# A transformer block on one core: the context as a tile of 128 and a doubled 64, queries and keys rounded ahead of the sums' inverse, both ends reordered

## The chip, the cores and the metric

The kernel runs on one core of one Trainium2 chip. The metric is the device time in microseconds (us) of one execution; a lower time is better. TensorE (PE) has a separate unit for its weight loads (PEld); VectorE is DVE, ScalarE is ACT, GpSimd is POOL, SyncE is SP.

## The reference

For 4 batch rows with 512 tokens of width 256, and a context of 512 tokens of width 192:

```python
attn_in = _adaln(x, cond, ln1_w, ln1_b, ...)
x = _attn(attn_in, attn_in, sa_wq, sa_wkv, sa_wo, sa_bo) + x      # self
cross_in = _adaln(x, cond, ln1_w, ln1_b, ...)
ctx_n = _ln(context, ca_lnc_w, ca_lnc_b)
x = _attn(cross_in, ctx_n, ca_wq, ca_wkv, ca_wo, ca_bo) + x       # cross
ffn_in = _adaln(x, cond, ln2_w, ln2_b, ...)
x = gelu(ffn_in @ ff_w1 + ff_b1) @ ff_w2 + ff_b2 + x
```

`_attn` has 16 heads of 64, rotates queries and keys by position, and takes a softmax over all 512 keys. All of it is float32.

## The kernel before, in words

Most products are made of float32r halves: an operand is written as a rounded high half and a low half (the difference), and a product is three matmuls, high by high, high by low and low by high (`parts`). Queries, keys, the normed activations, the context, the weights and the attention's output are split so. ACT writes the high halves (`high_qk`, `high_o`), DVE or POOL the low ones (`low_qk`, `low_o`, `norm_split`, `low_weights`).

The attention runs in 64 periods, one for each pair of heads of a batch row: two pairs of one batch row make a quad u, and 4 quads (one for each batch row) share one set of weights w. Quads 0 to 15 are self-attention (periods 0 to 31), quads 16 to 31 cross-attention. Each engine has its own hand-written order (`period(p)`), and semaphores tie them. In period p:

- PE scores pair p, four blocks of keys (`score`, L813 to L819: two row halves of the array, one for each head), and between the blocks multiplies queries and keys of pair p+1 for their row maxima (`peak`, L848); then the column sums of the exponentials of pair p-1 (`total`, L860), the average of the values for pair p (`average`, L872), and the projections for later pairs: one job of queries or keys (`project`, job p+4; even jobs are keys and fall in even periods), in odd periods the values of the next quad (`project_v`), in even periods the output projection of the quad that ended (`project_out`, which waits for `low_o(p-1)` of the same period).
- ACT takes the exponentials (L548), the inverse of the sums of pair p-1 by a logarithm and an exponential (`guess_inverse`, L554 and L556), the high half of queries and keys of pair p+2 (`high_qk`, L562), and the high half of the output of pair p-1 (`high_o`, L574).
- DVE takes the row maxima (L1065), corrects the inverse and multiplies (`normalise`, L1070 to L1075, which start once ACT has the inverse), writes the low half of that output (`low_o`, L1079), then the low half of queries and keys of pair p+2 (`low_qk`, L1083: both inputs in SBUF), the products with the rotation table (`rotate`, L1092) and the residual additions (L1109).
- POOL adds the exponentials of pair p (`add_probs`, L415 and twice L420: all in SBUF), does halves of weights and norms, additions of bias rows (`add_bias`, L437) and the rotation's sums (L429, L430). SP lands the rotated queries and keys by DMA (`land`) and the row maxima (`land_max`).

In cross-attention the 192 context channels are two tiles of 96 rows (CK = 96), so that a key job has 2 halves x 2 tiles x 3 = 12 matmuls of 512 columns, and a quad's values 4 x 2 x 3 = 24 matmuls of 256 columns. 16 layer norms (4 of the context) are strewn over the periods: statistics in one (L1050), rows in the next, transposes on PE in the one of `turned_in`. Ahead of the periods stand the first norms and projections, behind them the two-layer network (`mlp`) for the four batch rows.

## Time and profile before

| | |
|---|---|
| median of 3 runs | 1116.58 us (1114.38 to 1116.66) |
| profiled execution, its own time | 1118.88 us |
| its span | 1117.1 us |
| PE busy | 1097.2 us, 98% |
| DVE / POOL / ACT busy | 858.1 / 775.7 / 636.9 us |
| mean granted PE clock | 0.994 |

The span goes from the first to the last instruction of the profiled execution; its own time has 1.8 us more, for what lies around. A timeline gives each instruction, or a run of like ones, with its start and its length in us; in brackets stands how long the engine sat idle before it and what ended that. Lines of the kernel are written L813.

### The profile page before, as it was taken

How to read it: one execution, taken by the hardware profiler on the slowest of the kernel's cores; microseconds unless marked ns; L12 is line 12 of the kernel's file. 1: busy time of each engine (PE TensorE's matmuls, PEld its weight loads, DVE VectorE, ACT ScalarE, POOL GpSimd, SP SyncE). 2: the span in 40 equal slices, each digit the busy share in tenths (PEclk: the TensorE clock that was granted, in tenths of full speed). 3: DMA queues.
4: the chain of work that ended last, by engine and by line, in shares of the span. 5: the costliest groups of instructions: out<-in, count | busy, mean ns of one | idle time of the engine just before them, and what ended most of it. 6: DMA issues, size and time to landing. Idle time of an engine off the chain costs nothing.

```text
span 1117.1 us, 18312 instructions
## 1 busy us (share of the span) xinstructions
PE 1097.2 (98%) x6904; PEld 785.1 (70%) x6904; DVE 858.1 (77%) x1023; ACT 636.9 (57%) x895; POOL 775.7 (69%) x503
## 2 busy tenths in 40 slices
PE   8989999999999999999999999999999999989998
PEld 7657666776666776666766667766666776756997
DVE  5878887878787777878888777777877777788554
ACT  6465565665666555577665555555555545775521
POOL 2687887787788767789799766777777667755210
PEclk9899999999999999999999999999999999999999
DMA  6312121311231111211121112211121111300001
GB/s 175 86 46 57 32 53 39 89 30 30 53 77 38 39 36 23 72 39 39 29 63 38 39 39 59 51 23 36 38 72 39 37 31 30 114 1 1 20 19 38
DMA packets 59606, 52.31 MB, mean 47 GB/s; under 512 B 23040, under 2 KB 42496, under 8 KB 59264
## 3 DMA queue, kind: packets, MB, share of 16 engines
q1 hardware_dynamic: 57632, 49.57, 18.5%
q10 hardware_dynamic: 1888, 1.59, 0.5%
q8 instruction: 55, 0.90, 0.3%
q14 instruction: 31, 0.25, 0.1%
HBM read 15.22 MB, written 2.10 MB: 16 GB/s over the span
## 4 chain that ended last, share of the span: by engine, by line
PE 90%; DVE 5%; ACT 2%; issue 1%; DMA 1%; SPq 0%; POOL 0%; ACTq 0%; POOLq 0%; DVEq 0%
PE ps L872 18%; PE ps L713 12%; PE ps L715 11%; PE ps L714 11%; PE ps L813 6%; PE ps L860 6%; PE ps L848 5%; PE ps L819 5%; PE ps L815 5%; PE ps L817 5%; PE ps L963 4%; DVE lo L1083 1%; PE ps L729 1%; DMA x<-x_dram 1%; DVE w_lo L1117 1%
## 5 line engine op out<-in xcount | busy, mean ns | idle before, releaser
L548 ACT ACTIVATE probs<-ps 128x1024 f32<-128x1024 f32 x256 | 262.5, 1027 | 208.0 <-PE ps L819 183.6
L1065 DVE TENSOR_REDUCE neg_max<-ps 128x2 f32<-128x1024 f32 x256 | 301.6, 1226 | 76.7 <-PE ps L848 76.7
L420 POOL TENSOR_TENSOR acc<-acc,probs 128x1024 f32<-128x1024 f32 x128 | 306.2, 2392 | 18.6 <-POOL acc L415 0.4
L872 PE MATMUL ps<-probs,v 128*64 128x512 f32 x1024 | 230.7, 592 | 0.0
L415 POOL TENSOR_TENSOR acc<-probs 128x1024 f32<-128x1024 f32 x64 | 153.2, 2394 | 72.1 <-ACT probs L548 72.1
L872 PEld LDWEIGHTS ps<-probs,v 128*64 128x64 f32 x1024 | 73.9, 137 | 146.1 <-issue 146.1
L429 POOL TENSOR_TENSOR eo<-tmp 128x512 f32<-128x512 f32 x63 | 89.7, 1424 | 120.2 <-DVE tmp L1092 120.1
L1092 DVE TENSOR_TENSOR tmp<-ps,rope 128x1024 f32<-128x1024 f32 x126 | 148.2, 1211 | 4.5 <-PE ps L715 4.3
L813 PE MATMUL ps<-max_rows,pick 64*128 64x512 f32 x512 | 109.3, 419 | 2.6 <-DVE o_lo L1079 1.6
L713 PE MATMUL ps<-xn_hi,w_hi 128*128 128x512 f32 x256 | 107.8, 421 | 2.5 <-DVE o_lo L1079 1.3
L848 PE MATMUL ps<-hi 64*128 64x512 f32 x512 | 104.8, 400 | 5.4 <-DVE neg_max L1065 2.6
L819 PE MATMUL ps<-hi,lo 64*128 64x512 f32 x512 | 104.0, 396 | 0.0
L715 PE MATMUL ps<-xn_hi,w_lo 128*128 128x512 f32 x256 | 102.8, 402 | 0.0
L815 PE MATMUL ps<-hi 64*128 64x512 f32 x512 | 102.7, 392 | 0.0
L817 PE MATMUL ps<-lo,hi 64*128 64x512 f32 x512 | 102.4, 390 | 0.0
L714 PE MATMUL ps<-xn_lo,w_hi 128*128 128x512 f32 x256 | 102.0, 398 | 0.0
L1083 DVE TENSOR_TENSOR lo<-lo,hi 128x1024 fp32r<-128x1024 f32 x64 | 98.3, 1535 | 0.0
L1070 DVE SCALAR_TENSOR_TENSOR ps<-ps,inv 128x512 f32<-128x512 f32 x64 | 44.8, 700 | 68.6 <-ACT inv L556 68.6
L580 ACT COPY v<-ps 128x512 f32<-128x512 f32 x64 | 37.4, 589 | 100.5 <-PE ps L715 100.5
L848 PEld LDWEIGHTS ps<-hi 64*128 64x128 f32 x512 | 81.0, 306 | 17.8 <-issue 5.2
L430 POOL TENSOR_TENSOR eo<-tmp 128x512 f32<-128x512 f32 x63 | 81.3, 1291 | 0.0
L713 PEld LDWEIGHTS ps<-xn_hi,w_hi 128*128 128x128 f32 x256 | 49.0, 192 | 45.4 <-issue 33.9
(116 smaller groups left out, 2250.0 us busy)
## 6 DMA issues: line engine op xcount, KB each, us to landing
lo<-eo SPq DMA_DIRECT2D x126, 256.0 KB, 3.2
w_raw<-pack_dram SPq DMA_DIRECT2D x16, 192.0 KB, 3.9
x<-x_dram SPq DMA_DIRECT2D x4, 512.0 KB, 7.5
w_raw<-pack_dram SPq DMA_DIRECT2D x8, 256.0 KB, 4.3
max_rows<-neg_max SPq DMA_DIRECT2D x128, 2.0 KB, 2.0
w_raw<-w_dram SPq DMA_DIRECT2D x2, 1024.0 KB, 5.8
out<-x SPq DMA_DIRECT2D x8, 256.0 KB, 2.2
ctx_in<-ctx_dram SPq DMA_DIRECT2D x4, 384.0 KB, 4.2
```

Source lines behind the costliest of these rows:

```text
L420: pool.tensor_tensor(acc[:, g % 2, :, :], acc[:, g % 2, :, :], probs[:, i, :, :], ALU.add).then_inc(added, 1)
L548: act.activation(probs[:, i, :, :], score_ps(i), ACT.Exp, scale=SCALE).then_inc(exped, 1)
L713: pe.matmul(out, a_hi, b_hi, start=first, stop=False)
L714: pe.matmul(out, a_hi, b_lo, start=False, stop=False)
L715: return pe.matmul(out, a_lo, b_hi, start=False, stop=last)
L813: pe.matmul(out[:, h, :], pick[half[h], :], max_rows[half[h], :], start=True, stop=False)
L815: pe.matmul(out[:, h, :], k_hi[half[h], cut], q_hi[half[h], :], start=False, stop=False)
L817: pe.matmul(out[:, h, :], k_hi[half[h], cut], q_lo[half[h], :], start=False, stop=False)
L819: mm = pe.matmul(out[:, h, :], k_lo[half[h], cut], q_hi[half[h], :], start=False, stop=True)
L848: mm = pe.matmul(out[:, h, :], hi[half, g % 2, 0, cut], hi[half, g % 2, 1, :], start=True, stop=True)
L872: mm = pe.matmul(av_ps[DH * h:DH * h + DH, :], v[:, u % 2, kt, c:c + DH], probs[:, kt, h, :], start=(kt == 0), stop=(kt == TT - 1))
L1065: dve.tensor_reduce(neg_max[:, g % 2, :, i], peak_ps(i), AX.X, ALU.max, negate=True).then_inc(maxed, 1)
```

## The change

It does these things. (1) The context's 192 channels become one tile of 128 rows and one of 64; the 64 are laid down twice, at rows 0 to 63 and 64 to 127, so that two products with the 64 can stand in the two row halves of the array (`project_rest` for keys, ahead of `total`; `project_v_rest` for values, behind the other projections). Context norms have four more ACT instructions each, weights of cross-attention 11 loads in place of 7, and several PSUM banks are dealt out anew. (2) In every period ACT does `high_qk(p + 2)` ahead of `guess_inverse(p - 1)`, and DVE does `low_qk(p + 2)` ahead of `normalise(p - 1)`. (3) At the start job 3 is cut in four pieces between the maxima of pair 0 (`project_3`), `land_max(0)` goes ahead of `land(2)`, the low half of pair 1 moves to POOL, and the first four bias additions move to periods 13 to 21. (4) At the end the scores of pair 62 no longer wait for the output before them, the split of the network's weights is one DVE instruction for each matrix instead of four, and DVE takes one of the last additions of exponentials from POOL.

```diff
-LOADS = (5, 7)
+LOADS = (5, 11)
...
+        def is_wide(u):
+            return QUADS // 2 <= u < QUADS - 1
+
+        def v_ps(u, tt):
+            if is_wide(u):
+                return ps[:, ((6, 7), (2, 3))[tt % 2][tt // 2], 0:D]
+            return ps[:, (3 if u == QUADS - 1 else 5) + tt // 2, tt % 2 * D:(tt % 2 + 1) * D]
...
+        def av_ps(g):
+            return ps[:, 5 if g == PAIRS - 3 else 1, :]
...
+        def is_rest(j):
+            return j % 2 == 0 and j >= JOBS // 2
+
+        def out_ps(u, r):
+            if u == QUADS - 1:
+                return last_ps[r]
+            return ps[:, (3 if is_job(2 * u + 6) and is_rest(2 * u + 6) else 5, 6)[r], :]
...
-        bias_in.update({0: 0, 1: 1, 5: 2, 7: 3})
+        bias_in.update({13: 0, 15: 1, 18: 2, 21: 3})
...
+                        first, second = KT * 128, KT * 128 + 256
+                        for rows, kt, src, at in ((slice(0, CK), 0, slice(0, CK), first),
+                                                  (slice(CK, 128), 0, slice(0, 128 - CK), second),
+                                                  (slice(0, 64), 1, slice(128 - CK, CK), second),
+                                                  (slice(64, 128), 1, slice(128 - CK, CK), second)):
+                            sp.dma_start(raw[rows, 1:3, kt, a, :],
+                                         pack[src, at:at + 256].rearrange("p (m c) -> p m c", m=2))\
...
             land(1)
+            land_max(0)
             land(2)
-            land_max(0)
             load_x(3)
...
+            pool.wait_ge(qk_high, 2)
+            pool.tensor_tensor(lo[:, 1, :, :], raw_qk[:, 1, :, :], hi[:, 1, :, :], ALU.subtract).then_inc(qk_low_1, 1)
...
+                    if order[n][0] == C:
+                        act.activation(z[:, tt, DC:D], src[:, tt, 128:DC], ACT.Identity, bias=centre[:, tt:tt + 1],
+                                       scale=rstd[:, tt:tt + 1])
+                    act.activation(z[:, tt, 0:src.shape[-1]], src[:, tt, :], ACT.Identity, bias=centre[:, tt:tt + 1],
...
                         exp(p, i)
+                if is_pair(p + 2):
+                    high_qk(p + 2)
                 if is_pair(p - 1):
                     guess_inverse(p - 1)
                 if p in rows_in_period:
                     norm_rows(rows_in_period[p])
...
+            def project_rest(j):
+                w, b, _ = quad(j // 2)
+                pe.wait_ge(maxed, 4 * (j - 3) + 3)
+                pe.wait_ge(w_split, 4 * w + 1)
+                pe.wait_ge(ln_split, 2 * norm_of(C, 1, b) + 2)
+                for n, (w_, a_) in enumerate(((w_hi, ctx_hi), (w_hi, ctx_lo), (w_lo, ctx_hi))):
+                    for e, half in enumerate(halves):
+                        c = slice(256 + e * 128, 256 + (e + 1) * 128)
+                        pe.matmul(job_ps(j, e), w_[half, 1, c], a_[half, b, 1, :], start=(n == 0), stop=False)
...
+            def project_v(u):
...
+                    for kt in range(1 if phase == 1 else KT):
+                        c = slice(kt * 256, (kt + 1) * 256)
+                        for n, (a_, w_) in enumerate(((a_hi, w_hi), (a_hi, w_lo), (a_lo, w_hi))):
+                            mm = pe.matmul(v_ps(u, tt), a_[:, b, kt, cut], w_[:, 2, c],
+                                           start=first and kt == 0 and n == 0, stop=(phase == 0 and kt == KT - 1 and n == 2),
+                                           skip_group_check=True)
...
+            def project_v_rest(u):
+                b = quad(u)[1]
                 for t in range(2):
-                    cut = slice((2 * r + t) * 128, (2 * r + t + 1) * 128)
-                    for kt in range(KT):
-                        c = slice(kt * 256, (kt + 1) * 256)
-                        mm = parts(v_ps(u, r)[:, t * D:(t + 1) * D], a_hi[0:rows, b, kt, cut], a_lo[0:rows, b, kt, cut],
-                                   w_hi[0:rows, 2, c], w_lo[0:rows, 2, c], kt == 0, kt == KT - 1)
-                mm.then_inc(v_projected, 1)
+                    for n, (a_, w_) in enumerate(((ctx_hi, w_hi), (ctx_hi, w_lo), (ctx_lo, w_hi))):
+                        for r, half in enumerate(halves):
+                            cut = slice((2 * r + t) * 128, (2 * r + t + 1) * 128)
+                            mm = pe.matmul(v_ps(u, 2 * r + t), a_[half, b, 1, cut], w_[half, 2, 256:512],
+                                           start=False, stop=(n == 2), skip_group_check=True)
+                            if n == 2 and (t == 1 if not is_wide(u) else r == 1):
+                                mm.then_inc(v_projected, 1)
...
-                    if g > 0:
+                    if g > 0 and g != PAIRS - 2:
                         pe.wait_ge(av_kept, g)
-                    if g > 1:
+                    if g > 1 and g != PAIRS - 2:
                         pe.wait_ge(o_low, g - 1)
...
+                if is_job(p + 4) and is_rest(p + 4):
+                    project_rest(p + 4)
...
+                if p in v_in and quad(v_in[p])[2] == 1:
+                    project_v_rest(v_in[p])
...
+            project_v(0)
             project(2)
             modulate(2)
             peak(0, 0)
             peak(0, 1)
             modulate(3)
+            project_3(0, 0)
             peak(0, 2)
+            project_3(0, 1)
             peak(0, 3)
+            project_3(1, 0)
+            project_3(1, 1)
             norm(2, 0)
             norm(2, 1)
-            project(3)
...
+            def add_last_probs():
+                dve.wait_ge(exped, 4 * PAIRS)
+                dve.tensor_tensor(tmp[:, 0, :, :], probs[:, 2, :, :], probs[:, 3, :, :], ALU.add).then_inc(last_added, 1)
 
             def period(p):
                 u = p // 2
                 if is_pair(p + 1):
                     for i in range(TT):
                         peak(p + 1, i)
-                if p == 0:
-                    low_qk(1)
+                if is_pair(p + 2):
+                    low_qk(p + 2)
+                if p == PAIRS - 3:
+                    norm_stats(stats_in[p])
                 if is_pair(p - 1):
                     normalise(p - 1)
-                if p in stats_in and p != PAIRS - 3:
-                    norm_stats(stats_in[p])
+                if p == PAIRS - 1:
+                    add_last_probs()
+                if p in stats_in:
+                    if p != PAIRS - 3:
+                        norm_stats(stats_in[p])
                     norm_means(stats_in[p])
                 if is_pair(p - 1):
                     low_o(p - 1)
-                if p == PAIRS - 3:
-                    norm_stats(stats_in[p])
-                    norm_means(stats_in[p])
                 if p == PAIRS - 2:
-                    for c in range(4):
-                        split_ffw(0, c)
-                if is_pair(p + 2) and p not in stats_in:
-                    low_qk(p + 2)
+                    split_ffw(0)
                 if is_job(p + 4):
                     rotate(p + 4, 0)
                     rotate(p + 4, 1)
-                if is_pair(p + 2) and p in stats_in:
-                    low_qk(p + 2)
                 if p % 2 == 0 and is_quad(u - 1):
                     add_out(u - 1, 0)
                     add_out(u - 1, 1)
                 if p == PAIRS - 2:
-                    for c in range(4):
-                        split_ffw(1, c)
+                    split_ffw(1)
...
```

## Rows read from the trace of the kernel before

**Rows 1.** The page, the chain that ended last, shares of the span by engine.

```profile
PE 90%; DVE 5%; ACT 2%; issue 1%; DMA 1%; SPq 0%; POOL 0%; ACTq 0%; POOLq 0%; DVEq 0%
```

**Rows 2.** Timeline of PE, period 44: start us, us, line, tile, [idle before].

```profile
720.41 0.50 PE L813 MATMUL ps<-max_rows,pick 64*128 64x512 f32 x2
...
725.25 1.08 PE L860 MATMUL ps<-acc,ones 128*64 128x512 f32 x4
...
729.70 0.50 PE L713 MATMUL ps<-ctx_hi,w_hi 96*128 96x512 f32 x1
...
732.55 0.28 PE L713 MATMUL ps<-w_hi,o_hi 128*128 128x256 f32 x1
...
735.47 0.50 PE L813 MATMUL ps<-max_rows,pick 64*128 64x512 f32 x2
```

**Rows 3.** Timeline of ACT, DVE and POOL in the same period 44.

```profile
721.66 4.50 ACT L548 ACTIVATE probs<-ps 128x1024 f32<-128x1024 f32 x4 [0.56 <-PE ps L819]
...
726.38 0.60 ACT L554 ACTIVATE inv<-ps 128x512 f32<-128x512 f32 x1 [0.22 <-PE ps L860]
...
729.87 0.59 ACT L574 CAST o_hi<-ps 128x512 fp32r<-128x512 f32 x1 [0.69 <-DVE ps L1075]
...
721.89 4.70 DVE L1065 TENSOR_REDUCE neg_max<-ps 128x2 f32<-128x1024 f32 x4 [2.33 <-PE ps L848]
...
727.67 0.70 DVE L1070 SCALAR_TENSOR_TENSOR ps<-ps,inv 128x512 f32<-128x512 f32 x1 [1.08 <-ACT inv L556]
...
730.49 0.69 DVE L1079 TENSOR_TENSOR o_lo<-ps,o_hi 128x512 fp32r<-128x512 f32 x1 [0.65 <-ACT o_hi L574]
...
731.10 1.37 DVE L1083 TENSOR_TENSOR lo<-lo,hi 128x1024 fp32r<-128x1024 f32 x1
...
732.39 2.34 DVE L1092 TENSOR_TENSOR tmp<-ps,rope 128x1024 f32<-128x1024 f32 x2
...
726.47 2.38 POOL L420 TENSOR_TENSOR acc<-acc,probs 128x1024 f32<-128x1024 f32 x1
```

**Rows 4.** Timeline of POOL and DVE around 50 us, period 0.

```profile
49.89 2.36 POOL L420 TENSOR_TENSOR acc<-acc,probs 128x1024 f32<-128x1024 f32 x1
...
49.96 3.38 DVE L1083 TENSOR_TENSOR lo<-lo,hi 128x1024 fp32r<-128x1024 f32 x1
...
52.40 3.19 POOL L420 TENSOR_TENSOR acc<-acc,probs 128x1024 f32<-128x1024 f32 x1
```

**Rows 5.** Timeline of DVE and PE where PE waits for a lower half.

```profile
1000.50 0.69 DVE L1079 TENSOR_TENSOR o_lo<-ps,o_hi 128x512 fp32r<-128x512 f32 x1 [0.65 <-ACT o_hi L574]
...
1001.25 0.39 PE L713 MATMUL ps<-w_hi,o_hi 128*128 128x256 f32 x1 [0.42 <-DVE o_lo L1079]
```

**Rows 6.** Timeline, value projection of period 43, and weight loads (PEld).

```profile
717.43 0.28 PE L713 MATMUL ps<-w_hi,ctx_hi 96*128 96x256 f32 x1
...
720.20 0.28 PE L715 MATMUL ps<-w_hi,ctx_lo 96*128 96x256 f32 x1
...
720.40 0.19 PEld L813 LDWEIGHTS ps<-max_rows,pick 64*128 64x128 f32 x2
```

**Rows 7.** Timeline of SP and PE in periods 0 and 1.

```profile
38.30 1.77 SPq L354 DMA_DIRECT2D max_rows<-neg_max  x2
...
44.66 0.62 PE L848 MATMUL ps<-hi 64*128 64x512 f32 x2 [0.24 <-issue]
...
62.43 0.63 PE L848 MATMUL ps<-hi 64*128 64x512 f32 x2 [1.70 <-DVE neg_max L1065]
```

**Rows 8.** Timeline of DVE in period 59; the group of the bias additions.

```profile
956.45 1.40 DVE L1050 BATCH_NORM_STATS2 stats<-x 128x6 f32<-128x256 f32 x4
...
958.37 0.68 DVE L1079 TENSOR_TENSOR o_lo<-ps,o_hi 128x512 fp32r<-128x512 f32 x1
...
L437 POOL TENSOR_TENSOR x<-x,bias_rows 128x1024 f32<-128x1024 f32 x12 | 31.7, 2645 | 0.0
```

**Rows 9.** Timeline of PE, start of period 62.

```profile
989.46 0.50 PE L813 MATMUL ps<-max_rows,pick 64*128 64x512 f32 x2 [1.55 <-DVE o_lo L1079]
```

More of the change, by code:

```diff
@@ L735, in project @@
                 w, b, phase = quad(u)
-                pe.wait_ge(w_split, 4 * w + place[k] + 1)
-                pe.wait_ge(ln_split, 2 * norm_of(C if k == 1 and phase == 1 else X, phase, b) + 2)
-                if k == 1 and phase == 1:
-                    rows, a_hi, a_lo = CK, ctx_hi, ctx_lo
-                else:
-                    rows, a_hi, a_lo = 128, xn_hi, xn_lo
-                for e in range(2):
-                    if j in (1, 3):
-                        pe.wait_ge(roped, 2 * (j - 1) + e + 1)
-                    if j == 3 and e == 1:
-                        pe.wait_ge(maxed, 3)
-                    for kt in range(KT):
+                whole = not is_rest(j)
@@ L748, in project @@
+                if whole:
+                    pe.wait_ge(w_split, 4 * w + place[k] + 1)
+                    pe.wait_ge(ln_split, 2 * norm_of(X, phase, b) + 2)
+                a_hi, a_lo = (xn_hi, xn_lo) if whole else (ctx_hi, ctx_lo)
+                for e in range(2):
+                    if j == 1:
+                        pe.wait_ge(roped, e + 1)
+                    for kt in range(KT if whole else 1):
                         c = slice(kt * 256 + e * 128, kt * 256 + (e + 1) * 128)
-                        mm = parts(job_ps(j, e), w_hi[0:rows, k, c], w_lo[0:rows, k, c],
-                                   a_hi[0:rows, b, kt, :], a_lo[0:rows, b, kt, :], kt == 0, kt == KT - 1)
+                        mm = parts(job_ps(j, e), w_hi[:, k, c], w_lo[:, k, c], a_hi[:, b, kt, :], a_lo[:, b, kt, :],
+                                   whole and kt == 0, not whole or kt == KT - 1)
```

163 lines of the change are left out of this document (99 added, 64 removed).

## The prediction

> **What bounds the kernel now.** I read the chain that ended last first: nine tenths of it is TensorE [rows 1], so the kernel is as long as PE's queue, and any other engine counts only where PE waits for it. Then the timeline of PE in an ordinary even period, number 44 [rows 2]. It starts at 720.41 and the next at 735.47, 15.06 us. I count from its start: scores and peaks to 4.84, total and average to 9.29, 12 key matmuls to 12.14, 24 matmuls of the output projection and the turn to the next period 2.92. No idle time stands in a bracket there. Last the other engines in that period [rows 3], for how late they come. The lower half of the output, for which the projection at 12.14 waits, is ready at 10.77 (730.49 + 0.69 - 720.41), so that PE has 1.4 us in hand. DVE is idle for 1.08 us ahead of `normalise`; there the change puts `low_qk`.
>
> **The context's tiles.** A key job goes from 12 slots to 6 whole ones and 3 pairs. A slot of 512 columns costs 2.85 / 12 = 0.24 us [rows 2], turns of the array's shape included, and the score's row pairs show that a pair costs one slot: 20 of them in 4.84 us. The job gives back about 0.70 us in each of 16 even periods. It adds no turn of shape, since the pairs follow the peaks, which use the same row halves. But they reuse the banks of the third peak, whose reduction ends about 3.5 us into DVE's 4.70 us, at 5.05 [rows 3], 0.3 us after PE is there: 0.4 us net per even period, if PE is what ends it. The values of a quad, 24 slots in 2.98 us [rows 2, 6], 0.12 us each, go to 12 and 6 pairs. A pair of 256 columns is in no row. Two bounds: one slot for a pair, 0.12, which saves 0.72 us; or two, 0.24, if the two weight loads come one behind the other, which saves nothing. I take 0.12: the two loads of a score pair lie together in 0.19 us, as long as a single load's record [rows 6]. There are 15 such odd periods, 10.8 us in all; the values in period 60 are counted with that period below. The bound at the other end is 0.
>
> The Trainium skill (TensorE: Matmul & The Clock Gate, section LDWEIGHTS) puts a load at its columns over 1.2 GHz, 107 ns for 128; two loads in line would make a pair some 0.21 us and the saving 0.2 us by that estimate. The rows, with both loads inside 0.19 us, speak against loads in line, and no run here times a pair of 256.
>
> The other parts of this edit are off the path: four more ACT instructions per context norm cost some 1 us where ACT then waits for DVE, and four more weight loads fall on SP once in eight periods, with a period to spare.
>
> **Rounding ahead of the inverse.** On ACT it is nearly free: the exponentials end at 5.75 (721.66 + 4.50), the cast takes 1.0 us to 6.7, and the inverse, otherwise at 5.97, starts 0.7 us later. The price is on DVE. `low_qk` is then issued at about 6.75. POOL at that time is in the first of its two L420 additions, 6.06 to 8.44 [rows 3]. Period 0 shows what these two instructions do to each other [rows 4]: `low_qk` started 0.07 us after L420, took 3.38 us instead of about 1.2, and ended 1.09 us after L420 did (49.89 + 2.36 = 52.25; 53.34); the next L420 took 3.19 instead of 2.4 and ended late by what it had been held up. So one of them waits for the whole of the other. Period 44 agrees: where it now stands, `low_qk` meets only the last 0.3 us of POOL's additions and takes 1.37 us.
>
> The Trainium skill (SBUF — State Buffer, section Who interferes with whom) has the rule for it: a DVE instruction with two SBUF inputs and a GpSimd instruction that reads SBUF exclude each other for an instruction's length, and the one issued first wins. The trace agrees to a tenth of a microsecond. By the rule alone the end of `low_qk` would be that of the running addition and its own 1.2 us, 9.6, and the sum the same within 3 us.
>
> In the new place `low_qk` therefore ends at 8.44 + 1.09 = 9.53, not at 8.0, and `normalise` starts there instead of at 7.26. From its start to the end of the lower half are 3.51 us (727.67 to 731.18) [rows 3], so the half comes at 13.0. PE is at `project_out` at 12.14, or in cross-attention, with 0.4 us less ahead of it, at 11.7. It takes up work 0.06 us after such a half and the first matmul is 0.1 us longer (1001.19, 1001.25; 0.39 against 0.28) [rows 5]. The even period is then 13.0 + 0.16 + 2.92 = 16.1 us, whatever PE has to do before: 1.0 us more than 15.06, and what the key job saved is lost in the wait. Behind the waiting matmul stand PE's whole next period, and DVE's rotation, 2.3 us later, still in time for the next peaks. Odd periods have no output projection, and keep their length.
>
> Summed, in a first part (periods 2 to 26) and a second (28 to 60):
> - 5 ordinary even periods of the first part, +1.0 each: 5.0.
> - 4 behind which POOL first splits a context norm (8, 12, 16, 20): L420 is later, `low_qk` gets in behind L415: +0.3 each, 1.2.
> - 3 after a period with statistics (6, 10, 18). These push `low_o` back by 1.2 us [rows 8], on top of `low_qk`, so rotation, landing and the next additions come late: +1.9 each, 5.7. Period 14 has one of the moved bias additions, 2.4 us or more, ahead of its rotation as well [rows 8]: +3.0.
> - Second part: 12 ordinary ones +1.0 each, 12.0; four with transposes and statistics before (28 to 34) 2.6 together; period 60, 1.2.
>
> That is 30.7 us, against the values' 10.8.
>
> **Both ends.** At the start `land_max(0)` was issued at 38.30 [rows 7], and the maxima are there at 36.9; the first peak of pair 1 can come at about 41.9 instead of 44.66, when the rotation of job 3 is done. In period 1 a wait of 1.70 us for DVE goes, as the low half of pair 1 no longer stands in DVE's queue nor a bias addition in POOL's, and some time at the lower clock with it. I take 5.5 us, between 3 and 7, and 1.9 us for waits in periods 3, 7 and 15. At the end PE waited 1.55 us for `low_o(60)` [rows 9]. The wait moves to the first peak of pair 63, but `low_qk(63)` and 1.4 us of statistics now stand ahead of that output, about 3 us of which are new: I take +2; the single-instruction splits and the shared addition give back 1. So the end costs 1 us, between -3 and +3.
>
> The sum is 30.7 - 10.8 - 5.5 - 1.9 + 1.0 = +13.5 us, 1118.88 to 1132.4 for the profiled execution, whose time stands 2.3 us above the median; from the median, 1130.1.
>
> **The rivals.**
> - *The even periods don't wait.* If `low_qk` and POOL's additions pass each other (or `low_qk` slips in before L420), the half comes at about 11.9, where PE is. Then the key jobs save 16 x 0.4 = 6.4, less 2 for waking, the values 11.5 with period 60, the ends 5.5 + 1.9 + 2: 25 us less, 1091. For it: PE is 98% busy and `low_qk` fits DVE's idle 1.08 us. Against it: [rows 4].
> - *Value pairs cost two slots.* All else as forecast: +10.8, 1141.
> - *The landing comes late.* `high_qk(p + 2)` of even periods waits for a DMA from the period before. With odd periods shorter it would be ready at about 6.6, `low_qk` would be issued at 7.7, and until 8.44 nothing changes. Beyond that, by 0.8 us more, the second L420 goes first, and each such period costs 2.5 us more: in 15 periods 37 us, 1167.
> - *It ends near no change.* The even periods wait, but the start gives 7 and they cost 0.6 instead of 1.0: 1118.
>
> **How the numbers follow.** Forecast 0.62 (1118 to 1142 by itself); no wait 0.20; two slots 0.08; late landing 0.05; near no change 0.05. From 0.2% (2.2 us, about what a measurement of this kernel can tell from none) the first, third and fourth are slower nearly always, with 0.05 of them faster; hence faster 0.26, same 0.06, slower 0.68. The range takes part of the no-wait case and the two-slot one: 1096 to 1146.
>
> **What would show it.** In the profile after: `low_qk` at some 2.7 us in place of 1.5; a wait of `project_out` for the lower half of about 1.3 us in even cross-attention periods; even periods of 16.1 us, odd ones of 14.45 in cross-attention; one L420 in two at 3.4 us; the first period 2 to 3 us earlier. If `low_qk` stays at 1.3 us, the mechanism is wrong and the kernel faster. If value pairs start 0.24 us apart, their term is.

## The result and the profile after

The changed kernel takes 1137.35 us (median of 4 runs, 1136.76 to 1139.86), the kernel before, on the same chip, 1115.48 (1114.35 to 1116.66): ratio 1.020, 95% interval 1.018 to 1.022. It is slower, as forecast, by 21.9 us rather than 13.5; whether by more or less than 2% the interval leaves open. The profiled execution took 1136.76 us, its span is 1135.0 us.

First the chain that ended last, the line that answers to [rows 1]: PE holds two fifths of it in place of nine tenths, so on most of the way another engine was late.

```profile
PE 38%; POOL 19%; DVE 14%; issue 12%; ACT 9%; DMA 8%; SPq 0%; POOLq 0%; ACTq 0%
```

Next PE's waits: us in total, how many, the longest. The first is `project_out` waiting for the lower half of the output, the second the transposes for the rows of a norm, the third the first peak of pair 63.

```profile
PE ps L764 <- DVE o_lo L1192: 21.6, 23, 2.9
PE ps L780 <- ACT z L554: 5.8, 7, 1.5
PE ps L951 <- DVE o_lo L1192: 3.2, 1, 3.2
```

And the groups of GpSimd's added exponentials and of `low_qk`: instructions, then busy time and mean ns of one. They were 2392 and 1535 ns before.

```profile
L457 POOL TENSOR_TENSOR acc<-acc,probs 128x1024 f32<-128x1024 f32 x126 | 351.0, 2786 | 18.1
...
L1196 DVE TENSOR_TENSOR lo<-lo,hi 128x1024 fp32r<-128x1024 f32 x63 | 139.9, 2220 | 58.1 <-ACT hi L611 58.1
```

The timeline of period 44 answers to [rows 2] and [rows 3], its first rows to [rows 6]. The period starts at 730.92.

```profile
730.45 0.28 PE L854 MATMUL ps<-w_hi,ctx_lo 64*128 64x256 f32 x2
730.56 0.28 PE L854 MATMUL ps<-w_hi,ctx_hi 64*128 64x256 f32 x2
730.68 0.28 PE L854 MATMUL ps<-w_lo,ctx_hi 64*128 64x256 f32 x2
...
735.97 0.50 PE L814 MATMUL ps<-ctx_hi,w_hi 64*128 64x512 f32 x2 [0.16 <-DVE neg_max L1178]
...
736.94 5.69 POOL L457 TENSOR_TENSOR acc<-acc,probs 128x1024 f32<-128x1024 f32 x2
...
737.46 1.05 ACT L611 CAST hi<-lo 128x1024 fp32r<-128x1024 f32 x1 [0.81 <-DMA lo<-eo]
...
738.54 1.85 DVE L1196 TENSOR_TENSOR lo<-lo,hi 128x1024 fp32r<-128x1024 f32 x1 [1.45 <-ACT hi L611]
...
740.31 0.69 DVE L1183 SCALAR_TENSOR_TENSOR ps<-ps,inv 128x512 f32<-128x512 f32 x1
...
743.11 0.69 DVE L1192 TENSOR_TENSOR o_lo<-ps,o_hi 128x512 fp32r<-128x512 f32 x1 [0.65 <-ACT o_hi L623]
```

```profile
742.57 0.40 PE L766 MATMUL ps<-ctx_hi,w_lo 128*128 128x512 f32 x1
743.86 0.38 PE L764 MATMUL ps<-w_hi,o_hi 128*128 128x256 f32 x1 [0.89 <-DVE o_lo L1192]
...
746.79 0.49 PE L915 MATMUL ps<-max_rows,pick 64*128 64x512 f32 x2
```

What is to be seen: `low_qk` is issued at 7.6 us into the period, while the first L457 runs, and ends at 9.47; `normalise` starts there; the lower half ends at 12.88; PE's next matmul could start at 11.9 (742.57 and one slot of 0.23) and waits. The pairs of the value projection, a row for each pair (x2), start 0.12 us apart: one slot, as taken. Even periods of cross-attention take 15.87 us, odd ones 14.54 (15.06 and 15.17 before).

The end, timelines of DVE and PE, answers to [rows 9]:

```profile
1001.28 2.50 DVE L1196 TENSOR_TENSOR lo<-lo,hi 128x1024 fp32r<-128x1024 f32 x1 [0.53 <-ACT hi L611]
1003.70 1.39 DVE L1163 BATCH_NORM_STATS2 stats<-x 128x6 f32<-128x256 f32 x4
...
1007.81 0.69 DVE L1192 TENSOR_TENSOR o_lo<-ps,o_hi 128x512 fp32r<-128x512 f32 x1 [0.17 <-ACT o_hi L623]
```

```profile
1008.60 0.81 PE L951 MATMUL ps<-hi 64*128 64x512 f32 x2 [3.23 <-DVE o_lo L1192]
1009.18 0.66 PE L915 MATMUL ps<-max_rows,pick 64*128 64x512 f32 x2
```

After this wait a pair of matmuls takes 0.43 us instead of 0.23 until 1014: the granted clock is 0.50 from 1008 to 1014 and 0.73 over the stretch from 1010 to 1018. Period 62 takes 19.85 us (14.72 before).

To add up, I take the starts of periods 2, 28, 60 and 63 from PE's timeline (the first score). Every later table is in this form; all in us.

| | start of 2 | 2 to 28 | 28 to 60 | 60 to 63 | from 63 | span |
|---|---|---|---|---|---|---|
| before | 76.86 | 397.43 | 487.98 | 41.91 | 112.92 | 1117.1 |
| after | 71.55 | 410.74 | 492.17 | 49.56 | 110.98 | 1135.0 |
| difference | -5.3 | +13.3 | +4.2 | +7.7 | -1.9 | +17.9 |
| forecast | -5.5 | +13.0 | +3.8 | with the next | +2.2 | +13.5 |

The spans differ by 4 us less than the medians do. Experiment 11 shows most of the reason.

### The profile page after: what moved, and what is told of

It is laid out like the page before. It is cut to its first block, busy times and chain, and to the rows that moved or that the text cites. A ratio compares the mean times of both kernels' runs of the same rounds, so it can differ in the third digit from the quotient of the medians.

```text
span 1135.0 us, 18342 instructions
## 1 busy us (share of the span) xinstructions
PE 1085.8 (96%) x6908; PEld 764.3 (67%) x6908; DVE 895.5 (79%) x1017; ACT 637.3 (56%) x912; POOL 790.9 (70%) x502
## 4 chain that ended last, share of the span: by engine, by line
PE 38%; POOL 19%; DVE 14%; issue 12%; ACT 9%; DMA 8%; SPq 0%; POOLq 0%; ACTq 0%
DMA lo<-eo 7%; POOL acc L457 6%; PE ps L764 5%; DVE lo L1196 5%; PE ps L766 5%; PE ps L765 5%; PE ps L1076 4%; POOL acc L452 4%; POOL eo L467 3%; PE ps L915 3%; POOL eo L466 3%; PE ps L980 3%; ACT hi L611 3%; PE ps L921 2%; PE ps L917 2%
## 5 line engine op out<-in xcount | busy, mean ns | idle before, releaser
L457 POOL TENSOR_TENSOR acc<-acc,probs 128x1024 f32<-128x1024 f32 x126 | 351.0, 2786 | 18.1
L1196 DVE TENSOR_TENSOR lo<-lo,hi 128x1024 fp32r<-128x1024 f32 x63 | 139.9, 2220 | 58.1 <-ACT hi L611 58.1
L466 POOL TENSOR_TENSOR eo<-tmp 128x512 f32<-128x512 f32 x63 | 81.2, 1290 | 121.9 <-DVE tmp L1205 121.6
L623 ACT CAST o_hi<-ps 128x512 fp32r<-128x512 f32 x64 | 37.5, 587 | 164.6 <-DVE ps L1188 164.5
L951 PE MATMUL ps<-hi 64*128 64x512 f32 x512 | 109.6, 413 | 7.4 <-DVE o_lo L1192 3.2
L764 PE MATMUL ps<-xn_hi,w_hi 128*128 128x512 f32 x256 | 106.7, 417 | 2.2 <-DVE xn_lo L319 1.9
L917 PE MATMUL ps<-hi 64*128 64x512 f32 x512 | 104.5, 395 | 0.0
L951 PEld LDWEIGHTS ps<-hi 64*128 64x128 f32 x512 | 82.6, 306 | 21.5 <-issue 12.8
L764 PE MATMUL ps<-w_hi,o_hi 128*128 128x256 f32 x256 | 74.0, 289 | 21.3 <-DVE o_lo L1192 21.3
L467 POOL TENSOR_TENSOR eo<-tmp 128x512 f32<-128x512 f32 x63 | 81.5, 1293 | 0.0
L611 ACT CAST hi<-lo 128x1024 fp32r<-128x1024 f32 x64 | 66.6, 1041 | 24.0 <-DMA lo<-eo 22.2
```

The lines of the kernel that those rows point to most:

```text
L457: pool.tensor_tensor(acc[:, g % 2, :, :], acc[:, g % 2, :, :], probs[:, i, :, :], ALU.add).then_inc(added, 1)
L764: pe.matmul(out, a_hi, b_hi, start=first, stop=False)
L951: mm = pe.matmul(out[:, h, :], hi[half, g % 2, 0, cut], hi[half, g % 2, 1, :], start=True, stop=True)
L1196: dve.tensor_tensor(lo[:, g % 4, :, :], raw_qk[:, g % 4, :, :], hi[:, g % 2, :, :], ALU.subtract)\
```

## The experiments

**1 and 2: which of the two moves costs.** The first puts only DVE's order back, the second ACT's too; the tiles and both ends stay.

```diff
 # 1: DVE                                       # 2: as 1, and ACT
-                if is_pair(p + 2):
-                    low_qk(p + 2)              # ahead of normalise
...
+                if is_pair(p + 2) and p not in stats_in:
+                    low_qk(p + 2)              # behind low_o, as before
...
+                if is_pair(p + 2) and p in stats_in:
+                    low_qk(p + 2)              # behind rotate, as before
...
-                if is_pair(p + 2):             # 2 only: ahead of the inverse
-                    high_qk(p + 2)
...
                 if p in rows_in_period:
                     norm_rows(rows_in_period[p])
+                if is_pair(p + 2):             # 2 only: behind the inverse
+                    high_qk(p + 2)
```

> The changed kernel with DVE's low_qk(p + 2) put back behind low_o(p - 1) (behind rotate in periods with statistics), all else as changed, ACT's order too. Theory (low_qk and POOL's additions exclude each other, and the output's lower half comes late for the output projection): low_qk falls from 2.2 to about 1.35 us, even periods from 15.9 to 15.05 in self-attention and to about 14.7 in cross-attention, odd ones in cross-attention stay at 14.55, and the time is 1090 to 1098 us, 2% below the kernel before. Rival (the order on ACT, or the context's tiles and their banks, make the even periods late): even periods stay near 15.9 and the time near 1137 us.

> As the kernel with low_qk put back, and ACT's high_qk(p + 2) behind guess_inverse(p - 1) again. Theory: ACT's order alone is worth nothing or up to 0.1 us a period either way, so within 3 us of the kernel with low_qk alone put back (1090 to 1098 us). Rival (ACT's order has a part in the loss, since the cast waits for a DMA and the inverse waits behind it): 5 us or more below it.

Measured: 1123.22 us for the first (ratio 1.007, 1.005 to 1.010), 1108.32 for the second (0.994, 0.992 to 0.996). The first missed its expectation by 25 us. `low_qk` is at 1489 ns and L457 at 2377 (63 and 126 instructions), so the two hardly meet any more; what is left is ACT's order. Period 14 of the first shows it; rows of its timeline:

```profile
265.69 1.05 ACT L611 CAST hi<-lo 128x1024 fp32r<-128x1024 f32 x1 [1.91 <-DMA lo<-eo]
...
272.00 0.69 DVE L1192 TENSOR_TENSOR o_lo<-ps,o_hi 128x512 fp32r<-128x512 f32 x1 [1.90 <-ACT o_hi L623]
...
272.75 0.38 PE L764 MATMUL ps<-w_hi,o_hi 128*128 128x256 f32 x1 [2.36 <-DVE o_lo L1192]
```

`high_qk` waits 1.91 us for a DMA that lands late, and the inverse, the rows of a norm and the rounding of the output, none of which needs that DMA, wait behind it. (Part of PE's wait of 2.36 us is the norm itself: in run 2 the same period has a wait of 0.67.) Over the whole of run 1 ACT's casts wait 23 us for landings, and PE 8.2 us for the rows of norms. Taken back one after the other, the two moves give 14.1 and 14.9 us: 1137.4, 1123.2, 1108.3.

**3: the order alone, on the kernel before.** The lines that go from the old places are left out here.

```diff
 # ACT                                          # DVE
+                if is_pair(p + 2):
+                    high_qk(p + 2)             # ahead of guess_inverse
...
+                if is_pair(p + 2):
+                    low_qk(p + 2)              # ahead of normalise
```

> The kernel before with part 2 of the change alone: ACT's high_qk ahead of guess_inverse and DVE's low_qk ahead of normalise. Theory: 28 even periods longer by 0.85 us, those behind statistics by 1 to 2 us, some 3 us at the end: 1144 to 1152 us. Rival (the order costs only together with the new tiles or banks): within 5 us of 1116.

Measured: 1154.04 us (ratio 1.034, 1.033 to 1.036), 39 us more than before. Its groups:

```profile
L420 POOL TENSOR_TENSOR acc<-acc,probs 128x1024 f32<-128x1024 f32 x128 | 356.0, 2781 | 18.7 <-POOL acc L415 0.4
...
L1083 DVE TENSOR_TENSOR lo<-lo,hi 128x1024 fp32r<-128x1024 f32 x64 | 155.8, 2436 | 49.2 <-ACT hi L562 49.2
```

Its ordinary even periods take 15.9 us, as the changed kernel's do, with the longer key job: what PE has to do before the wait doesn't enter. The whole change is then this +39 and some -17 for tiles and ends.

**4: take away what `low_qk` meets.** GpSimd's L457 additions become writes of ones into the same sums, behind the same waits; the exponentials of two of four key blocks are left out of the sums.

```diff
-                    pool.tensor_tensor(acc[:, g % 2, :, :], acc[:, g % 2, :, :], probs[:, i, :, :], ALU.add).then_inc(added, 1)
+                    pool.memset(acc[:, g % 2, :, :], 1.0).then_inc(added, 1)
```

> The changed kernel, its orders untouched, with POOL's two additions L420/L457 of a period replaced by a write of ones into the same sums, so that POOL is at work but reads nothing from SBUF when low_qk comes; this leaves the exponentials of two of four key blocks out of the sums. Theory (what low_qk waits for is POOL's reading of SBUF): low_qk takes 1.1 to 1.3 us at its new place, the lower half is ready about 11.8 us into an even period, and the time falls to 1088 to 1098 us. Rival (any instruction of POOL holds DVE up, or the place in DVE's queue is what costs): low_qk at 1.8 us or more, or even periods still near 15.9 us.

Measured: 1105.62 us (0.991, 0.989 to 0.993), 32 less than the changed kernel with both moves in place. The groups:

```profile
L457 POOL MEMSET acc<- 128x1024 f32 x126 | 119.9, 952 | 15.0
L1196 DVE TENSOR_TENSOR lo<-lo,hi 128x1024 fp32r<-128x1024 f32 x63 | 77.4, 1229 | 39.4 <-ACT hi L611 39.4
```

Even periods take 15.04 and 14.78 us: the waits are gone. The time came out above the 1088 to 1098 expected, since periods 14 and 62 still take 17.03 and 17.67. This run also shortens two of GpSimd's three instructions on the sums of a period; it doesn't separate the exclusion from GpSimd's load. The next one does.

**5: the same GpSimd work, `low_qk` issued 1.2 to 1.7 us later.** ACT's order is put back, DVE's is left as changed.

```diff
-                if is_pair(p + 2):
-                    high_qk(p + 2)
                 if is_pair(p - 1):
                     guess_inverse(p - 1)
                 if p in rows_in_period:
                     norm_rows(rows_in_period[p])
+                if is_pair(p + 2):
+                    high_qk(p + 2)
```

> The changed kernel with ScalarE's order put back (the two activations of the inverse ahead of the rounding of the pair after next) and VectorE's left as changed (low_qk ahead of normalise). Theory (VectorE and GpSimd's additions exclude one another, so that a low_qk which meets an addition ends behind it): low_qk can now start only at some 9.2 us into the period (in the run with both orders back the rounding lasts from 8.16 to 9.2), inside the second addition (8.6 to 11.0 of the period); it ends at some 12.1, the three steps of normalise at 14.3, the lower half at 16.2, and TensorE, which needs it at some 12, waits 4: plain even periods of 18 to 19.5 us in both parts in place of 15.9, so some 3 us times 31 more than the changed kernel: 1210 to 1240 us. Rival (low_qk costs only its own duration of 1.2 to 2.2 us ahead of normalise, wherever it starts, and the run with VectorE's order back and ScalarE's as changed lost its 15 us to ScalarE's order): putting ScalarE's order back gains those 15 us here too, some 1122 us, even periods near 15.9 or less.

Measured: 1246.91 us (2 runs; ratio 1.117, 1.113 to 1.121), above the expected range, and 125 us from the rival. Rows of the timeline of an even period of cross-attention (from 797.64):

```profile
803.66 4.87 POOL L457 TENSOR_TENSOR acc<-acc,probs 128x1024 f32<-128x1024 f32 x2
...
806.95 2.66 DVE L1196 TENSOR_TENSOR lo<-lo,hi 128x1024 fp32r<-128x1024 f32 x1 [3.13 <-ACT hi L611]
...
813.08 0.39 PE L764 MATMUL ps<-w_hi,o_hi 128*128 128x256 f32 x1 [3.39 <-DVE o_lo L1192]
```

and of one of self-attention, number 24 (from 446.22):

```profile
452.26 5.72 POOL L457 TENSOR_TENSOR acc<-acc,probs 128x1024 f32<-128x1024 f32 x2
...
454.43 1.29 DVE L1196 TENSOR_TENSOR lo<-lo,hi 128x1024 fp32r<-128x1024 f32 x1 [2.01 <-ACT hi L611]
...
459.19 0.38 PE L764 MATMUL ps<-w_hi,o_hi 128*128 128x256 f32 x1 [0.60 <-DVE o_lo L1192]
```

In the first, `low_qk` is issued inside the second addition (803.66 + 4.87 = 808.53) and ends 1.08 us after it; the additions are not slowed, but GpSimd's next instructions are (L327, 2.40 us for two in place of 1.41). In the second it is issued 0.2 us ahead of the seam between the two, slips in, takes 1.29 us, and it is POOL that is slowed (5.72 for two instead of 4.87). Such a period takes 15.9 us, no more than in the changed kernel, although `low_qk` was issued 1.2 us further on (8.2 us into the period for 7.0). So the end of `low_qk` isn't set by when it is issued, but by the end of the addition that runs then. All rows of both profiles say so: in the changed kernel 56 of 63 `low_qk` start while an addition of exponentials runs, in experiment 5 55, and each of them ends 1.08 or 1.09 us after that addition. The 4.1 us by which the first period is longer than the changed kernel's are 2.5 from the half (15.4 us into the period for 12.9) and 1.6 from the clock: behind the wait of 3.39 us PE runs at half clock from 814 to 817, at 0.21 a matmul for 0.12. My expectation had neither that nor the ordinary self-attention periods right, where nothing is lost; those behind a norm take 20 to 24 us.

**6: the end's statistics.** They go back behind the lower half.

```diff
-                if p == PAIRS - 3:
-                    norm_stats(stats_in[p])
                 if is_pair(p - 1):
                     normalise(p - 1)
...
-                if p in stats_in:
-                    if p != PAIRS - 3:
-                        norm_stats(stats_in[p])
+                if p in stats_in and p != PAIRS - 3:
+                    norm_stats(stats_in[p])
                     norm_means(stats_in[p])
...
                     low_o(p - 1)
+                if p == PAIRS - 3:
+                    norm_stats(stats_in[p])
+                    norm_means(stats_in[p])
```

> The changed kernel with only the layer-norm statistics of the third last pair's period put back behind the lower half. Theory: the statistics (1.3 us on VectorE, 1003.70 to 1005.02) stand ahead of normalise there and make the lower half late for TensorE's first peak of the period before the last, where it waited 3.23 us and then ran at half clock until 1014; without them the wait is some 1.9 us and period 62 falls from 19.85 to 16.5 to 18.5 us; time 1 to 3.5 us less than the changed kernel: 1133.5 to 1136.5 us. Rival: the rows of that layer norm come late instead, and TensorE waits for its transposes in the same period: no gain, 1136.5 to 1139.

Measured: 1138.49 us over 5 runs, 1133.4 to 1142.6; no gain in time. In its profile the wait of L951 is shorter, and the clock stays at 1.00 behind it; from its waits:

```profile
PE ps L951 <- DVE o_lo L1192: 1.9, 1, 1.9
```

Behind it stands a new wait, for the exponentials, in the timeline of PE:

```profile
1009.18 0.50 PE L915 MATMUL ps<-max_rows,pick 64*128 64x512 f32 x2 [1.50 <-ACT probs L597]
```

Period 62 takes 17.86 us instead of 19.85. A gain of up to 2 us is seen there, in a profile of the fastest of the five runs, and none in times that scatter by 9 us: unclear.

**7: the weight loads.** The kernel of experiment 2 has one period out of line, number 34, at 18.95 us. Rows of SyncE's queue there:

```profile
573.09 0.71 SPq L350 DMA_DIRECT2D w_raw<-pack_dram  x1
...
579.93 0.60 SPq L361 DMA_DIRECT2D w_raw<-pack_dram  x1
580.62 1.18 SPq L389 DMA_DIRECT2D max_rows<-neg_max  x2
```

The edit issues five of the eleven loads one period earlier.

```diff
+                if p % 8 == 0 and NP // 2 <= p // 8 + 1 < NP:
+                    w = p // 8
+                    sp.wait_ge(w_split, 4 * w + 3)
+                    load_weights(w + 1, (0,))
...
-                    load_weights(w + 1)
+                    load_weights(w + 1, (0, 1) if w + 1 < NP // 2 else (1,))
```

> The changed kernel with both orders back (the kernel that took 1108.32 us) and the eleven weight loads of a cross-attention set issued in two periods: five at the first of a set's eight periods, six at the second. Theory: the 18.95 us of period 34 there are 3.9 over its neighbours because the maxima's two transfers were issued at 580.62, behind eleven weight loads that SyncE issued from 573.09 to 579.93; with five of them moved a period forward the maxima are issued some 3.2 us earlier and period 34 comes to 15.5 to 16: the time is 2.5 to 3.5 us less, 1104.8 to 1106.2 us. Rival: the period waits for something else that is late (the rotated keys, which GpSimd delivered 2.3 us late behind a layer norm's steps): it gains under 1 us, 1107.5 to 1108.5.

Measured: 1108.92 us (6 runs, 1106.5 to 1110.5; 1108.32 before the edit). No gain. Periods 34, 35 and 36 take 17.02, 15.46 and 16.07 us in place of 18.95, 14.53 and 15.08, in sum the same 48.6. And the kernel of experiment 8, which has no such edit, shows 17.24, 15.21 and 16.09. The loss is something else's; what of it is left open here, experiment 10 takes up in part.

**8: the four pieces of the start.** The kernel of experiment 2 with the pieces back behind the transposes.

```diff
             peak(0, 0)
             peak(0, 1)
             modulate(3)
-            project_3(0, 0)
             peak(0, 2)
-            project_3(0, 1)
             peak(0, 3)
-            project_3(1, 0)
-            project_3(1, 1)
             norm(2, 0)
             norm(2, 1)
+            for e in range(2):
+                for kt in range(2):
+                    project_3(e, kt)
```

> The changed kernel with both orders back (1108.32 us) and the four pieces of the fourth projection put back behind the transposes of the last layer norm of the start, where the kernel before has the whole projection. Theory: the start's gain of 5 to 6 us by the third period comes in large part from these pieces lying inside the waits of the first peaks for their maxima (12 matmuls, some 4.2 us at 32.7 to 37.1): without that the rotation of that job, the keys of pair 1 and its peaks come some 2.5 to 4 us later, the third period starts at 72.5 to 74.5 in place of 70.26, and the time is 1110.5 to 1112.5 us. Rival: the gain is from the moved rounding, the lower half of pair 1 on GpSimd and the earlier issue of the maxima, and the pieces were hidden anyway: third period at 70.3 to 71, time 1108 to 1109.

Measured: 1107.28 us (4 runs, 1106.6 to 1108.4; 0.992, 0.990 to 0.994), not slower than the 1108.32. The rival was right: period 2 starts at 70.51 (70.26 with the pieces between). They gain nothing that is seen.

**9: the moved biases alone, on the kernel before.**

```diff
-        bias_in.update({0: 0, 1: 1, 5: 2, 7: 3})
+        bias_in.update({13: 0, 15: 1, 18: 2, 21: 3})
...
+                if sublayer == 0:
+                    pool.wait_ge(o_added, 2 * (NB + b) + 2)
...
-                if r == 0:
+                if r == 0 and u >= 2 * NB:
                     dve.wait_ge(biased, NB * phase + b + 1)
```

The changed waits make a moved addition follow the residual additions to the same rows, where it used to come ahead of them.

> The kernel before with only the additions of the first sublayer's biases moved from periods 0, 1, 5 and 7 to 13, 15, 18 and 21. Theory: part of the start's gain of 5 to 6 us is this: in the kernel before, the lower half of a pair starts on VectorE at 57.80 beside GpSimd's bias addition at 57.77 and takes 3.43 us (1.3 alone), and the maxima behind it make TensorE wait 1.70 us at 62.43; without the bias there the lower half ends 2.2 us earlier and period 1 falls from 21.58 to 17.5 to 19.5 us: third period at 73 to 75 us in place of 76.86, time 1 to 4 us less, 1111.5 to 1114.5 us. Rival: the start's gain is from the moved rounding and the lower half of pair 1 on GpSimd alone; third period at 76 to 77, time within 1 us of before.

Measured: 1115.47 us against 1115.02, ratio 1.000, 0.999 to 1.001 (11 and 15 runs). Its profile shows what the theory said: `low_qk` 1.21 us instead of 3.43, no wait of 1.70 us in period 1, period 2 at 73.14 instead of 76.86. The time shows nothing of these 3.7 us. This contradiction led to experiment 11; against the second profile that it took, the start gains 1.6 us, not 3.7, period 7 gains 0.4, and periods 15 and 19, with waits of PE of 0.56 and 1.14 us for DVE, give back 2.0.

**10: the rest's pairs behind the total.** The kernel of experiment 8, with two lines exchanged on PE.

```diff
+                if is_pair(p - 1):
+                    total(p - 1)
                 if is_job(p + 4) and is_rest(p + 4):
                     project_rest(p + 4)
-                if is_pair(p - 1):
-                    total(p - 1)
```

> The kernel of 1107.28 us (both orders back, the four start pieces behind the transposes) with the pair of context products of the rest issued behind the total of the exponentials, not ahead of it. Theory: ahead of it they wait for the last but one maximum, 0.2 to 0.5 us in 15 periods, 3.1 us in sum in the run with the loads split; behind the total that maximum is there, and the time is 2 to 3 us less: 1104 to 1105.5 us. Rival: the total then waits in their place for the last sum or the last exponential: under 1 us less, 1106.3 to 1107.8.

Measured: 1099.95 us (4 runs, 1098.8 to 1100.9), ratio 0.987, 0.985 to 0.988: the best kernel of the study, 7.3 us under that of experiment 8, more than twice what was expected. The chain of its page:

```profile
PE 91%; ACT 4%; DVE 2%; issue 1%; DMA 1%; POOL 1%; SPq 0%; ACTq 0%; POOLq 0%
```

Ordinary even periods of cross-attention take 14.58 us instead of 14.78, which makes 2.2 us for the 11 from period 38 on and is what was expected; periods 30 to 36 take 106.7 instead of 111.3 us together, which was not. The pairs ahead of the total also held up the total, and so the inverse and what hangs on it; which of these frees periods 30 to 36 wasn't traced and stays open.

**11 and 12: both kernels once more, unchanged.**

> The kernel before once more, unchanged, for a second profile. In its first profile, of an execution of 1118.88 us, period 1 takes 21.58 us, with a granted clock of 0.81 to 0.85 from 60 to 70 us; with the biases moved it took 17.90 at full clock and the profiled execution 1115.26 us, and yet the medians of the two kernels are the same to 0.5 us. Reading A: the clock's fall in period 1 belongs to some executions only; another execution near the median shows period 1 at 18 to 19.5 us and the third period at 73.5 to 74.8 us, and the moved biases gain next to nothing. Reading B: period 1 takes 21.5 us in every execution; then the third period starts at 76.9 again, and the moved biases' gain in the start is given back in a place that their one profile does not show.

> The changed kernel once more, unchanged, timed beside the kernel before on the chip of this job. It settles whether the kernel with the statistics of period 61 put back (1138.49 us median, spread 1133.4 to 1142.6) gained anything. Theory: it gained 1 to 3 us in period 62, and the spread hid it: this kernel's median comes out at 1138.5 to 1141 us here. Rival: no gain: 1136.5 to 1138.5 us, as in its first runs (1136.76 to 1139.86).

Measured: 1115.3 us (8 runs, 1114.5 to 1116.4) and 1138.01 us (4 runs, 1135.3 to 1139.7). Beside both the kernel before ran as the control, 13 times, with a median of 1118.01 (1114.2 to 1119.3): two medians of the same kernel on one chip, 2.7 us apart. Over all controls of this study and experiment 11 its 58 times fall into two groups, 42 from 1113.9 to 1116.7 and 16 from 1117.5 to 1119.3; the first profile, of 1118.88, is from the upper one, the second, of 1115.53, from the lower. Against the control beside it the changed kernel loses 20.0 us (ratio 1.019, 1.016 to 1.022).

Experiment 12 answers experiment 6: no gain there that a median shows. For experiment 11, from the windows of PE in the kernel before, first the profile of the start of this study, then the new one (us, busy, instructions, granted clock, share of the DMA engines, GB/s):

```profile
60.00:65.00 5.00, 3.31 (x22) 0.81 0.03 7
```

```profile
60.00:65.00 5.00, 3.30 (x22) 1.00 0.14 29
```

The wait of 1.70 us is in both, the fall of the clock behind it in one. With the clock up, period 1 takes 20.00 us instead of 21.58, and period 2 starts at 74.73: reading A, though period 1 isn't as short as it said. Of the 3.4 us between the two profiles 2.1 lie ahead of period 2 and 1.3 behind period 63: there the first profile has a second stretch at half clock (0.50 from 1019 to 1022), the new one none. The changed kernel is worse in this. In its second profile PE waits 3.02 us for a rotation in period 1 (0.81 in the first):

```profile
58.03 0.82 PE L951 MATMUL ps<-hi 64*128 64x512 f32 x2 [3.02 <-DVE tmp L1205]
58.62 0.66 PE L915 MATMUL ps<-max_rows,pick 64*128 64x512 f32 x2
```

A pair takes 0.43 us from there to 64, and period 2 starts at 76.53 instead of 71.55. From period 2 on the two profiles differ by 2.7 us only: 1.3 in period 14, where PE waits 2.90 us in the first and 2.87 in the second, and the granted clock behind it is 0.50 (277 to 280) in the first and 1.00 in the second, and 0.9 in periods 60 to 62.

| | start of 2 | 2 to 28 | 28 to 60 | 60 to 63 | from 63 | span |
|---|---|---|---|---|---|---|
| before, second profile | 74.73 | 396.83 | 488.53 | 41.96 | 111.65 | 1113.7 |
| after, second profile | 76.53 | 409.08 | 492.06 | 48.64 | 110.99 | 1137.3 |
| 1, DVE's order back | 71.05 | 408.98 | 484.79 | 45.48 | 110.90 | 1121.2 |
| 2, both back | 70.26 | 401.95 | 481.11 | 41.66 | 110.92 | 1105.9 |
| 3, order alone | 79.07 | 406.28 | 508.60 | 46.64 | 111.71 | 1152.3 |
| 4, memset | 71.23 | 399.36 | 473.78 | 45.88 | 110.95 | 1101.2 |
| 10, rest behind total | 71.25 | 400.74 | 472.41 | 41.66 | 110.94 | 1097.0 |

## Why it came out so

**The mechanism held, to a tenth of a microsecond.** `low_qk` ahead of `normalise` was to meet the first of the two additions, to end 1.09 us behind it, at 9.53 us into the period, and to bring the lower half at 13.0. Period 44 shows 9.47 and 12.88, although `low_qk` was issued at 7.6 and not at 6.75: inside the same addition that makes no difference. Experiment 3 shows the cost without the tiles, experiment 4 that it goes with the additions, experiment 5 that it is set by the addition which runs at the issue: issued 1.7 us later, inside the second addition, the half comes 2.5 us later; issued 1.2 us later but still inside the first, no later. The Trainium skill (SBUF — State Buffer, section Who interferes with whom) states this exclusion, and that a GpSimd instruction which only writes SBUF doesn't take part in it. The traces agree with both: `low_qk` ends at 809.61, 1.08 us behind the addition, and takes 1229 ns where memsets stand in the additions' place.

**Even periods: 15.87 instead of 16.1.** 12 ordinary ones of the second part cost 10.6 us where I had 12.0, the 5 of the first part 4.5 for 5.0. Each has 0.1 us less up to the half and 0.1 less for waking. The four behind which POOL first splits a context norm cost nothing (1.2 forecast). The waits of periods 3, 7 and 15 give back 1.5 us for 1.9, nothing of it in 15. Periods 28 to 34 cost 3.7 for 2.6. The key job gives back less than the 0.4 us taken, 0.3 in experiment 2 (14.78 for 15.07); in the changed kernel the wait hides it.

**Odd periods: 14.54.** A pair of 256 columns costs one slot. 15 of them gain 10.1 us for 10.8; the two-slot rival is out.

**"On ACT it is nearly free" was wrong.** I looked only at the cast's own microsecond. Where a landing is late, everything behind `high_qk` in ACT's order waits for a DMA that it doesn't need: run 1 against run 2 prices that at 15 us when nothing else is in the way. In the changed kernel most of it lies under DVE's wait, and it came into the sum by other names. Periods 6, 10 and 18, which I had priced together at 5.7, measure 5.7, and that is partly luck: I had put it to VectorE's statistics, and what ends last there is ACT's queue. In period 6 `high_qk` waits 0.89 us for its landing, the inverse, the eight row instructions of the context norm and a weight's cast follow without a gap, and the lower half waits 1.39 us for the rounding of the output behind them. Period 14 has a wait of 2.45 us for the landing, behind the moved bias addition, and costs 4.6 us for the 3.0 forecast; in the second profile, with the clock up, it costs 3.3. The forecast had the late landing only as a rival with its own effect through GpSimd, not as one that holds up the inverse.

**"Off the path" was wrong for the context norms.** Their four more ACT instructions were entered at nothing. With both orders back (experiment 2) periods 6, 10, 14 and 18 take 15.93, 15.48, 15.95 and 15.47 us where the kernel before takes 15.03, 2.7 us together; in periods 6 and 14 the lower half waits 2.85 us for ACT, and PE 0.67 us for the lower half. In the kernel before it waits up to 1.53 us for ACT in the same periods, and PE never.

**The end: mis-sized.** Periods 60 to 62 cost 7.7 us (6.7 in the second profile) and the part behind gives back 1.9: +5.7 for a forecast of 1.2 and +1.0. The wait moved to L951 as said, and its size was about right: 3.2 us, 1.7 more than the 1.55 it replaces, for the 2 taken. But the clock is down behind it: at half clock 12 pairs cost 2.4 us more. With the statistics back (experiment 6) the wait is 1.9 and the clock stays up. Period 60 costs 2.1 us for 1.2, with a wait of PE of 1.55 us for the rows of a norm, which are ACT's. I had priced the wait and not what follows it. Of the 1.9 given back behind period 63, 1.3 are the first profile's second stretch at half clock; against the second profile it is 0.7.

**The start: right against one profile, wrong against the time.** The forecast of -5.5 met the profile's -5.3. But the kernel before had the clock's fall in its profiled execution, 1118.88 us, and at 1115.5 it mostly doesn't; and the changed kernel's start varies by 5 us itself. The four starts (76.86 and 74.73; 71.55 and 76.53) allow anything from -5.3 to +1.8 us. The medians say a little more: they differ by 21.9 us, and from period 2 on the profiles differ by 20.5 to 24.5. By this estimate the start gives 2.6 us at most, and may cost 1.4; two medians of the kernel before that lie 2.7 us apart make it a rough one. Of its edits the pieces gain nothing (8) and the biases nothing in time (9).

**The 7.3 us that are missing.** Two terms were mis-sized. The first is the start, where the profiled execution was taken for the median run: the medians differ by 4.0 us more than the two profiled spans, and the first profile's two stretches at half clock are most of it. The second is the end, +5.7 for 2.2. The rest of the sum came out 0.9 us higher in all (13.3 for 13.0, 4.2 for 3.8, 5.3 for 5.5), period 14's 1.6 being offset by the even periods. These make 8.4, and the kernel before's median, 1115.48 for the 1116.58 from which I counted, takes 1.1 off: 7.3 between 1130.1 and 1137.35.

**What would have been the better change.** The tiles and both ends with the order of before (2) give 6.7 us, and with the pairs behind the total (10) 15.1, each against the kernel before measured beside it: from 28 to 60 the second saves 15.6 of the 22.0 us that the slots promised (16 x 0.70 + 15 x 0.72): ordinary even periods give 0.5 us, odd ones 0.6.

## What to carry to other kernels

- Ahead of moving a VectorE instruction with two SBUF inputs, look at what GpSimd does at the time of its issue: if that one reads SBUF too, the VectorE instruction ended 1.1 us behind it here, so 1.2 us of shift cost nothing and 1.7 us cost 2.5. Look for a gap of GpSimd, not of VectorE.
- An instruction that waits for a DMA belongs behind those that don't, even if its own time is small; price the wait for the whole queue behind it.
- Where one profiled execution stands 0.3% above the median, find the place that differs before a saving there is entered in the sum. Here a second profile of the same kernel showed it.

## What the runs showed of the hardware

- PE's granted clock is at half (1.2 of 2.4 GHz) behind some waits and not behind others of like length: behind 1.70 us in period 1 of the kernel before it was 0.81 (60 to 65 us) in one execution and 1.00 in another; behind 2.9 us in period 14 of the changed kernel 0.50 (277 to 280) in one and 1.00 in the other. Behind 3.23 us it was 0.50 (1008 to 1014), behind 3.39 us at 813.1 in experiment 5 0.50 (814 to 817), and behind 1.9 us in experiment 6 1.00. So the same kernel had executions with and without such a stretch.
- VectorE's `low_qk` beside a GpSimd memset of the same size (952 ns) takes 1229 ns, as alone (1.22 at the start); issued inside an addition it takes 1.2 to 3.4 us, by how much of the addition is left, and ends 1.08 or 1.09 us behind it. A memset can stand in for an addition where one wants to see what the exclusion costs.
- Two matmuls of 64 rows and 256 columns in the two row halves start every 0.12 us, a pair at a time, as a single one of 128 rows does.
